# First attention of a two-layer block, chunks 1 to 3: split key and query rows spread through DRAM, fp32r scores, earlier feature maps

## What is computed

```python
q = (x @ Wq.T).reshape(B, L, H, D)        # H = 16 heads of D = 8
k = (x @ Wk.T).reshape(B, L, H, D)
v = (x @ Wv.T).reshape(B, L, H, D)
phi_q = jax.nn.elu(q) + 1.0
phi_k = jax.nn.elu(k) + 1.0
...
S = S + pk_t[..., :, None] * v_t[..., None, :]
z = z + pk_t
num = jnp.einsum('bhd,bhde->bhe', pq_t, S)
den = jnp.sum(pq_t * z, axis=-1, keepdims=True) + EPS
```

## Time and profile before

| | |
|---|---|
| median of 3 runs | 596.78 us (596.27 to 600.56) |
| the profiled execution | 592.93 us, span 591.2 us from the first to the last instruction |
| busy | PE 534.2 us (90%), DVE 435.1 (74%), ACT 338.3 (57%), POOL 317.5 (54%) |
| first attention alone | from the first L902 to the first expert product, about 16.5 to 121.7 us |

### The profile page before, as it was taken

How to read it: one execution, slowest core, us unless ns; L and a number is a source line. 1 busy time by engine, 2 the same in 40 slices (tenths; PEclk the granted TensorE clock), 3 DMA queues, 4 the chain that set the end, 5 groups by cost and what they waited for, 6 DMA issues and landing times.

```text
span 591.2 us, 11857 instructions
## 1 busy us (share of the span) xinstructions
PE 534.2 (90%) x3949; PEld 402.2 (68%) x3949; DVE 435.1 (74%) x1067; ACT 338.3 (57%) x575; POOL 317.5 (54%) x315
## 2 busy tenths in 40 slices
PE   4778897879999999999788888888899999999996
PEld 3556665657888888888444554555587888888884
DVE  3665668848889798668776687888668797796563
ACT  3473565356555555665545567666766655655553
POOL 4695887546665766677420202211156666666664
PEclk9998998999999999999898899999999999999999
DMA  6111200233353334335641343320042354344350
GB/s 172 30 43 41 82 2 2 74 85 97 105 112 122 125 94 126 89 113 190 197 126 37 98 145 98 126 73 2 9 122 87 114 131 136 90 146 127 89 150 25
DMA packets 42502, 56.60 MB, mean 96 GB/s; under 512 B 5953, under 2 KB 18258, under 8 KB 42450
## 3 DMA queue, kind: packets, MB, share of 16 engines
q1 hardware_dynamic: 39344, 55.46, 32.0%
q10 hardware_dynamic: 3106, 0.48, 0.4%
HBM read 47.27 MB, written 8.65 MB: 95 GB/s over the span
## 4 chain that ended last, share of the span: by engine, by line
PE 69%; ACT 10%; DVE 8%; issue 6%; POOL 4%; DMA 2%; SPq 1%; POOLq 0%; DVEq 0%; ACTq 0%
PE bank L814 17%; PE bank L816 16%; PE bank L815 16%; ACT PT L713 6%; PE bank L923 4%; PE bank L978 4%; DVE PT L1386 3%; PE bank L955 3%; PE bank L902 3%; ACT XN L771 1%; PE bank L1039 1%; PE bank L903 1%; PE bank L1014 1%; POOL WL L580 1%; DVE MEXP L1406 1%
## 5 line engine op out<-in xcount | busy, mean ns | idle before, releaser
L608 POOL TENSOR_TENSOR KS<-PT,QS 128x512 fp32r<-128x512 f32 x144 | 186.1, 1293 | 115.6 <-ACT QS L796 103.6
L791 ACT ACTIVATE bank<-bank 128x512 f32<-128x512 f32 x128 | 74.5, 582 | 98.9 <-PE bank L816 98.3
L1508 DVE TENSOR_TENSOR PT<-CS,bank 128x512 f32<-128x512 f32 x128 | 87.4, 683 | 45.2 <-PE bank L816 44.6
L814 PE MATMUL bank<-XH,WH 128*128 128x512 f32 (+1 forms) x288 | 115.0, 399 | 1.4 <-DVE PT L1386 1.4
L816 PE MATMUL bank<-XH,WL 128*128 128x512 f32 (+1 forms) x288 | 112.4, 390 | 0.0
L815 PE MATMUL bank<-XL,WH 128*128 128x512 f32 (+1 forms) x288 | 112.1, 389 | 0.0
L1406 DVE TENSOR_REDUCE MEXP<-bank 128x4 f32<-128x1024 f32 x64 | 78.1, 1224 | 30.5 <-PE bank L923 30.4
L796 ACT ACTIVATE QS<-PT 128x512 fp32r<-128x512 f32 x144 | 90.1, 626 | 12.2 <-DVE PT L1513 11.7
L1513 DVE TENSOR_TENSOR PT<-PT,bank 128x512 f32<-128x512 f32 x128 | 88.0, 687 | 9.5 <-ACT bank L791 1.6
L713 ACT ACTIVATE PT<-bank 128x1024 f32<-128x1024 f32 x64 | 65.5, 1024 | 49.0 <-PE bank L955 48.9
L978 PE MATMUL bank<-PT,V 128*32 128x256 f32 (+1 forms) x1024 | 65.6, 376 | 0.8 <-ACT PT L713 0.7
(11 more groups left out here) (179 smaller groups left out, 807.1 us busy)
## 6 DMA issues: line engine op xcount, KB each, us to landing
CS<-combine_rows SPq DMA_DIRECT2D x128, 256.0 KB, 3.2
head_rows<-HP SPq DMA_DIRECT2D x16, 256.0 KB, 3.0
QS<-head_rows SPq DMA_DIRECT2D x16, 256.0 KB, 2.7
KS<-head_rows SPq DMA_DIRECT2D x16, 256.0 KB, 3.0
head_rows<-PHI SPq DMA_DIRECT2D x8, 256.0 KB, 3.2
out_dram<-X SPq DMA_DIRECT2D x4, 256.0 KB, 3.8
stage<-in_L_ffn_gate_w_dram SPq DMA_DIRECT2D x5, 192.0 KB, 2.7
stage<-in_L_ffn_up_w_dram SPq DMA_DIRECT2D x5, 192.0 KB, 3.4
```

Source lines behind the costliest of these rows:

```text
L608: pool.tensor_tensor(GL[:, (u - 1) % 3, :], GG[:, (u - 1) % 3, :], GH[:, (u - 1) % 3, :].bitcast(f32), ALU.subtract).then_inc(F.gl, 1)
L791: act.activation(TH[:, u, :] if u < SHARED else G[u % 3][:, :], G[u % 3][:, :], ACT.Silu).then_inc(F.th, 1)
L814: pe.matmul(out, wh, vh, start=start, stop=False)
L1508: dve.tensor_tensor(ab, CS[:, e % CBUFS, :], U[u % 3][:, :], ALU.mult).then_inc(F.b, 1)
```

## The change

- `PQ` shrinks to one chunk. Chunk 0 keeps its fp32 products. For chunks 1 to 3 the map is written back into `PHI`; ACT makes its rounded high part in `HP` (`high_rows`), POOL the low part in `PHI` (`first_low`), SP writes both to `head_rows` and reads 24 rows for a head into `QS` and `KS` (`first_rows`); `products` waits for those loads and uses fp32r operands of 24 rows. The 12 `head_keys` of chunks 1 to 3 are gone.
- PE projects in slots 5, 6 / 12, 13 / 19, 20; ACT and DVE follow one slot later, POOL two slots later.
- The constant rows are made in slot 2 and written before all else; the loads of pieces 2 to 5 now stand on SP behind the rows of a chunk. DVE's reduction for `EIGHTH` moves ahead of the first norm.

```diff
         FIRST_SLOT = [0, 2]
         PROJECTION_SLOT = {2: 0, 4: 1}
+        FEATURE_SLOT = {0: (0, 0)}
+        for c, n in ((1, 5), (2, 12), (3, 19)):
+            FEATURE_SLOT[n], FEATURE_SLOT[n + 1] = (0, c), (1, c)
...
+            def first_rows(c):
+
+                A = AT[0]
+                for w in range(2):
+                    sp.wait_ge(A.hi, 2 * (c - 1) + w + 1)
+                    write_rows(A, c, w, False)
+                    sp.wait_ge(A.lo, 2 * (c - 1) + w + 1)
+                    write_rows(A, c, w, True)
+                sp.wait_ge(A.qw, 16 * (4 + 6 * c))
+                for j in range(HG):
+                    if c > 1:
+                        sp.wait_ge(A.s1, 4 * (SLOTS * (c - 1) + 2 * j + 2))
+                    for w, t in enumerate((QS, KS)):
+                        sp.dma_start(t[:, j, :].bitcast(f32),
+                                     spread[w, c % 2, j:H:HG].rearrange("h s c t -> h (s c) t")).then_inc(A.qr[j], 16)
...
+            piece(0)
+            piece(1)
+            constant_rows()
+            for c in range(1, CHUNKS):
+                first_rows(c)
+                if c < CHUNKS - 1:
+                    piece(2 * c)
+                    piece(2 * c + 1)
...
+            def first_low(w, c):
+
+                pool.wait_ge(AT[0].hi, 2 * (c - 1) + w + 1)
+                pool.tensor_tensor(PHI[:, w, :].bitcast(f32r), PHI[:, w, :], HP[:, w, :].bitcast(f32),
+                                   ALU.subtract).then_inc(AT[0].lo, 1)
...
-                    if cur and 2 <= g < 2 + HG:
-                        head_keys(g - 2)
+                    if 2 <= n < 2 + HG:
+                        head_keys(n - 2)
...
+                    if n >= 7 and n - 2 in FEATURE_SLOT:
+                        first_low(*FEATURE_SLOT[n - 2])
...
+                def high_rows(w, c):
+
+                    act.wait_ge(A.ph, 2 * c + w + 1)
+                    if w == 0 and c == 1:
+                        act.wait_ge(A.kx, HG)
+                    act.activation(HP[:, w, :], PHI[:, w, :], ACT.Copy).then_inc(A.hi, 1)
...
-                    k0, q0 = SEQ * b, cc * CHUNK + SEQ * b
-                    pe.wait_ge(A.kx, HG * cc + j + 1)
+                    k0, q0 = SEQ * b, SEQ * b
+                    if cc:
+                        pe.wait_ge(A.qr[j], 32 * cc)
+                        keys, queries, depth = KS, QS[:, j, :], 3 * HD
+                    else:
+                        pe.wait_ge(A.kx, j + 1)
+                        keys, queries, depth = KX, PQ[:, :], 32
...
-                    if g == 7 and c + 1 < CHUNKS:
-                        features(0, c + 1)
-                    if g == 0 and 0 < c < CHUNKS:
-                        features(1, c)
+                    if n and n in FEATURE_SLOT:
+                        features(*FEATURE_SLOT[n])
```

More of the change, by code:

```diff
@@ L251, in hybrid_block @@
         s_bc = sem("broadcasts_loaded")
-        s_raw = [sem(f"piece{p}_loaded") for p in range(PIECES)]
+        s_raw = [sem(f"pieces_loaded{p}") for p in range(2)]
         s_wh = sem("piece_high_done")
@@ L269, in hybrid_block @@
         LN = [NormSems(sem, f"ln{k}_", k != 2) for k in range(4)]
-        AT = [AttentionSems(sem, f"at{k}_", k) for k in range(2)]
+        s_rows_read = [sem(f"head_rows{j}_loaded") for j in range(4)]
+        AT = [AttentionSems(sem, f"at{k}_", k, s_rows_read) for k in range(2)]
         s_row_buffer = [sem(f"combine_row{i}_loaded") for i in range(CBUFS)]
@@ L382, in piece @@
[L382 to L390, removed]
+                        sp.dma_start(dst[:, n:UPP, k, :], w.rearrange("d (a f) -> d a f", a=2)).then_inc(s_raw[p % 2], 16)
@@ new lines, in piece, with constant_rows, write_rows @@
+                    sp.dma_start(dst[:, n:UPP, 2, :], sh_down.rearrange("(a f) d -> f a d", a=2)).then_inc(s_raw[p % 2], 16)
+            def constant_rows():
+                sp.wait_ge(s_cr, 1)
+                for r in range(2):
+                    for w, t in enumerate((QS, KS)):
+                        sp.dma_start(spread[w, r, :, 3, :, :], t[:, 0, :].bitcast(f32)).then_inc(AT[0].qw, 16)
+            def write_rows(A, c, w, low):
+                for part in (2 - w,) if low else (0, 1 + w):
+                    sp.dma_start(spread[w, c % 2, :, part, :, :], PHI[:, w, :] if low else HP[:, w, :].bitcast(f32))\
+                      .then_inc(A.qw, 16)
@@ L392, in spread_rows @@
             def spread_rows(c):
[L394 removed]
+                A = AT[1]
                 for w in range(2):
                     sp.wait_ge(A.px, 2 * c + w + 1)
[L397 to L398 removed]
+                    write_rows(A, c, w, False)
                     sp.wait_ge(A.lo, 2 * c + w + 1)
[L400 removed]
@@ L734, in slot @@
                     output()
-                    if n < ITEMS and g < 2:
-                        features(g)
+                    if n < 2:
+                        features(n, 0)
+                    elif n - 1 in FEATURE_SLOT:
+                        features(*FEATURE_SLOT[n - 1])
                     if n == 1:
@@ L756, in slot @@
                         qk_high()
+                    if n >= 6 and n - 1 in FEATURE_SLOT:
+                        high_rows(*FEATURE_SLOT[n - 1])
                 else:
@@ L1263, in _ @@
             dve.tensor_reduce(HEADS[:, :], BLOCKS[:, :, :], AX.X, ALU.add).then_inc(s_cd, 1)
+            dve.wait_ge(s_id, 2)
+            dve.tensor_reduce(EIGHTH[:, :], ident[:, 0:P:HD], AX.X, ALU.add).then_inc(s_cd, 1)
             first_apply()
@@ L1388, in masked_scores, with features @@
                                       .broadcast_to([P, 3, 3 * P]), ALU.mult).then_inc(A.mk, 1)
-                def features(w):
+                def features(w, c):
                     dve.wait_ge(A.rl, 2 * c + w + 1)
-                    if w and c:
-                        dve.wait_ge(A.kx, HG * c)
-                    dve.scalar_tensor_tensor(out=PK if w else ch(PQ, c, CHUNK), in0=PHI[:, w, :], scalar=1.0,
+                    dve.scalar_tensor_tensor(out=PHI[:, w, :] if c else PK if w else PQ[:, :], in0=PHI[:, w, :], scalar=1.0,
                                              in1=(MT if w else PJ)[:, :], op0=ALU.min, op1=ALU.add).then_inc(A.ph, 1)
```

58 lines of the change are left out of this document (29 added, 29 removed).

## The result

| | before | after |
|---|---|---|
| median | 598.67 us (4 runs, 596.27 to 601.84) | 614.72 us (4 runs, 613.66 to 616.43) |
| ratio | | 1.0285 (95% interval 1.0226 to 1.0345) |
| profiled execution | 592.93 us | 615.49 us |
| span, mean granted clock | 591.2 us, 0.980 | 613.7 us, 0.939 |

The changed kernel is slower by 2.9%, some 17 us by the ratio. Ratios here are taken from executions in the faster of two states that the chip shows, medians from all executions, so the two need not divide out exactly. 595.2 us had been forecast with a range of 588 to 602, so the forecast was wrong by 19.5 us and the time lies outside its range.

What follows compares the result with a forecast made beforehand. In the first attention the bound was taken to change by slot: PE-DVE ring, PE, POOL or DVE. Running differences +2.5, +4.3, +1.7 ended at -1.6 us, so 596.8 - 1.6 = 595.2 us, range 588 to 602.

Steps and rivals of the forecast that it cites:

- the products start 3.35 us after the first read: First attention, rows read back from DRAM: delay from first read to score products, taken from the second attention's reads.
- The score products: PE, first attention: eight fp32r products pass to the next step in 0.45 us instead of 0.89, saving 0.44 an item.
- ring: PE and DVE taking turns in the first attention's quiet slots: 2.54 us an item falls by 0.35 to 2.19.
- Rival C: Score products on PE: narrow fp32r products no faster than fp32 ones, time 598.7 us; chance 0.10.
- The first rows of chunk 1: POOL's low part done at 41.4, reads follow, item 8 at 47.8 us against 45.29 before: +2.5 us.
- Item 18: First attention, after piles on ACT and POOL: starts at 80.1 us against 75.84 before, +4.3, the worst point.
- Item 24: First attention, after a lighter pile in chunk 3: starts at 98.4 us against 96.67 before, +1.7.
- First expert product: End of the forecast chain, behind the first attention: 120.2 us against 121.74 before.
- The sum: Whole chain: +2.5, then +4.3, then +1.7, at the end -1.6 us, for a median of 595.2 us.
- B: Late low parts on POOL make items 8, 16 and 24 wait for reads at a low clock: 602.7 us; chance 0.16.
- slack: Argument against B: by the forecast's chain the reads of chunks 2 and 3 have time to spare.
- A: First attention's piles on ACT and POOL are softer than the chain, so the ring's gain comes through: 588.4 us; chance 0.22.

Runs made afterwards that it cites:

- experiment 1: Changed kernel with heads 4j to 4j+3 in group j for chunks 1 to 3, so a read's 128 rows lie in one piece: 599.69 us, ratio 1.0025 to before.
- Experiment 2: Changed kernel, strided reads kept, weight pieces 2 to 5 loaded from ACT's queue instead of SP's: 614.79 us in one execution.
- experiment 4: Changed kernel without row writes and reads of chunks 1 to 3, QS and KS filled once with constants: 592.39 us in one execution.
- experiment 8: Changed kernel without row writes and reads, constant QS and KS, weight pieces in slots 10, 12, 17, 19, 23, 25: 592.78 us once; over six 588.73, ratio 0.9874 to before.
- experiment 7: Kernel before with only the weight pieces moved to slots 10, 12, 17, 19, 23, 25: 595.59 us once; over twelve 592.77 against 596.77, ratio 0.9935.
- experiment 3: experiment 1 with the maps of chunk 2 two slots later and of chunk 3 one slot later: 602.56 us in one execution.

## Why the prediction was wrong

**The step that failed** is "the products start 3.35 us after the first read, as 284.63 did after a read begun at 281.28". It took the landing time of one read from a read of the same bytes and another shape. Measured: 8.73 us, and 3.85 us once experiment 1 gives the read the shape of the row. The reads were taken for a copy of the second attention's, while the diff shows `j:H:HG` and a view of three dimensions. All else follows from it: "Rows of chunk 2 arrive at about 71.4 before item 16 could start, so they cost nothing" (first read issued at 76.19, product at 84.19, after a wait of 3.57) and "Rows of chunk 3 landed at about 95" (item 24 waited 4.71 us, until 117.51).

**A second omission** has the same root. Of a moved step every issue counts, and eight reads and the pieces behind them share SP; I priced SP at nothing. In after, ACT's WH waits 9.1 us for pieces that SP could not issue in time. Experiment 2 shows that this was not a cause of its own: with those waits nearly gone the time stayed at 614.79.

**Point by point**, with the read repaired (experiment 1) the forecast's chain can be held against a run:

- The score products: 0.45 forecast, 0.39 measured; ring 2.19 forecast, 2.06 measured. Rival C (narrow fp32r products as dear as fp32) falls.
- The first rows of chunk 1: POOL done at 41.4 forecast, 40.2 measured in experiment 1 (38.95 + 1.27); item 8 at 47.8 forecast, 46.90 measured.
- POOL without idle time from 60 to 76: so in experiment 1; in after it idled 3.2 to 3.6 us before three of the masks there. The XN of chunk 0 near 76: 74.74 there, 85.17 in after.
- Item 18 at 80.1: 78.70. Item 24 at 98.4: 99.03. First expert product at 120.2: 122.11, 1.9 us late, since the tail took 23.1 us where my sum had 21.8, at a granted clock of 0.77 from 100 to 120 us; item 24 again waits for DVE (2.29 us), which I had expected to be over. The forecast held the shared port only against the low parts. In experiment 1 two routing steps stand beside a WL instead: SC takes 2.37 us and PMX 1.39, where before has 0.34 and 0.23, some 3.2 us of DVE's time in front of item 24. What that costs the kernel no run isolates.
- DVE's small steps: T, 1.01 us beside a KS before, takes 0.22 in after, as expected.
- The sum for a read of the right width was -1.6 us; experiment 1 measured +1.5 (-1.1 to +4.0), so even then the sum lies half a us outside.

**The rivals.** B named the right place, waits for rows at items 8, 16 and 24 with a low clock behind each, and the wrong cause: it wanted the low parts to be late, and in after chunk 1's was early. Chunk 2's was late there (its last write went out at 73.39, in experiment 1 at 63.79), but as a result of chunk 1's slow reads. Its price, 3 x (1.2 + 1.3) us, was far under what came: DMA waits of 7.4, 3.6 and 4.7, ACT waits of 8.9 in all, and a clock of 0.66 to 0.74. The "slack" that was put against B was computed with the same 3.35 us, so one wrong number fed both the forecast and its defence. A (the piles are soft) falls too: even with no round trip PE waited 6.4 us for POOL's masks in the old piece slots (experiment 4), and 1.7 us in the new ones (the single execution of experiment 8).

Where the 22.5 us of the profiled pair lie: 18.2 before the first expert product; of the other 4.3, 3.7 in the second attention (143.0 to 146.7 us), where the clock was 0.50 and 0.67 from 310 to 330 us. PE's program is the same there, and experiment 7 puts such a difference within what executions of one program show. The 143.0 us of before is also, with experiment 4, the shortest of all fourteen profiles of this case (143.0 to 149.8), and its execution lay below its median: the pair's 22.5 us hold some luck of before's profile, and the 17 us of the ratio are the better size.

## What to carry to other kernels

Before a DMA's time is borrowed from another row, compare the two access patterns dimension by dimension, not only bytes and names: with an outer dimension of 4 SP spent 2.46 us on the issue of a 256 KB read, with one of 128 it spent 0.43. Such a queue showed as a flat rate at a round share (25%) and as issue times of 2.4 us, and the loads behind it on the same issuer were late as well. When a change buys cheaper work on one engine with steps on others, first look where the long steps of those others stand: moving four of the six weight pieces by two or three slots gave the kernel before 3.9 us, where the new scores with the repaired read gave nothing that can be told.

## What was unexpected of the hardware

- SP's issue of a DMA is not a fixed cost: 0.43 us for a 256 KB read of 128 contiguous rows, some 2.46 us for one of the same size with an outer dimension of 4, after four quick ones (0.51 to 0.88 us). The issues then come every 2.51 us, at the pace of the transfers (101 GB/s).
- Four reads of 64 KB need 1.81 us to issue against 0.43 for one of 256 KB, so cutting a transfer up did spread it (share 49.1%), but made SP's issues the limit.
- Eight fp32r score products of 24 rows, half of them with 128 columns, took 0.39 us, where fp32 ones of 32 rows took 0.89.
- DVE's 128x64 TENSOR_SCALAR took 2.35 us beside a POOL WL of 2.65 and 0.23 in experiment 3, with no WL beside it.
- Two profiles of one program differed by 2.65 us at the first expert product, already by item 3 and at a granted clock of 1.00 in both, and by 3.9 us in a later stretch of the same code, where the clock was 0.50 and 0.50 in one and 0.64 and 0.83 in the other from 290 to 310 us.
